# Twelve decoder layers: layer 0 in two stages instead of four, semaphores cleared seldom, layer 11's scores on row groups

## What is computed

```
y   = norm(x)                                   # (x - mean) / sqrt(var + 1e-5)
a   = norm(y) * ln1_g + ln1_b
q, k, v = a @ wq, a @ wk, a @ wv                # 16 heads of 8
phi(t)  = elu(t) + 1
kv, z   = sum_s phi(k) v^T, sum_s phi(k)        # per head
res = y + ((phi(q) kv) / (phi(q) z + 1e-6)) @ wo
h   = norm(res) * ln2_g + ln2_b
r   = clip(round((h @ w1) / 0.1), -128, 127) * 0.1
x   = x + res + gelu(r) @ w2                    # w1: 128 x 512
```

## Time and profile before

| | us |
|---|---|
| median of three runs | 2183.69 |
| lowest, highest | 2175.89, 2206.31 |
| the profiled execution | 2188.4 |
| its span, first to last instruction | 2186.6 |
| mean granted TensorE clock in it | 0.927 |
| layer 0, first to last instruction (timeline) | 13.05 to 123.24 |
| layer 11, first stage (timeline) | 2116.95 to 2179.35 |

### The profile page before, as it was taken

One profiled execution on the slowest core, in us unless ns is written; L12 is line 12 of the kernel. 1 busy time (PEld: TensorE's weight loads), 2 busy tenths in 40 slices (PEclk: granted clock), 3 DMA queues, 4 the chain that ended last, 5 costly groups with the idle time before them and its releaser, 6 DMA issues. The chain is left out here.

```text
span 2186.6 us, 51110 instructions
## 1 busy us (share of the span) xinstructions
PE 1934.8 (88%) x20189; PEld 1383.8 (63%) x20208; DVE 1409.9 (64%) x2480; ACT 1149.8 (53%) x2426; POOL 859.9 (39%) x1103
## 2 busy tenths in 40 slices
PE   4888999986657999999999877999899989999786
PEld 2435787862445688888888753788788856633332
DVE  3654887774575677777776433788778757934434
ACT  3444555554376766666665434555555551066452
POOL 0001454420144576656566200666566630044100
PEclk8998999997577999999999988999999988989898
DMA  6000110000001200000000040544344400000100
GB/s 279 1 1 1 50 39 30 30 10 0 1 1 58 108 23 13 22 13 22 13 22 23 13 184 4 145 127 132 114 126 129 132 30 1 1 1 1 43 1 21
DMA packets 31955, 107.54 MB, mean 49 GB/s; under 512 B 9440, under 2 KB 9568, under 8 KB 30816
## 3 DMA queue, kind: packets, MB, share of 16 engines
q1 hardware_dynamic: 30624, 104.07, 14.1%
q10 hardware_dynamic: 1088, 0.13, 0.0%
HBM read 94.16 MB, written 10.03 MB: 48 GB/s over the span
## 5 line engine op out<-in xcount | busy, mean ns | idle before, releaser
L600 PE MATMUL bank<-yh,wl 128*128 128x512 f32 x640 | 253.8, 396 | 15.2 <-DVE yl L1300 6.8
L602 PE MATMUL bank<-yh,wh 128*128 128x512 f32 x640 | 252.3, 394 | 0.0
L601 PE MATMUL bank<-yl,wh 128*128 128x512 f32 x640 | 251.9, 394 | 0.0
L1867 DVE SCALAR_TENSOR_TENSOR big<-bank,pack,big 128x256 f32<-128x256 f32 (+2 forms) x384 | 182.2, 477 | 34.2 <-ACT mask L1789 16.8
L1353 DVE TENSOR_TENSOR hl<-bank,hh 128x512 fp32r<-128x512 f32 x192 | 132.9, 692 | 68.5 <-ACT hh L1290 58.8
L1788 ACT ACTIVATE big<-bank,pack 128x256 f32<-128x256 f32 x192 | 91.1, 474 | 135.0 <-PE bank L1623 134.4
L1290 ACT ACTIVATE hh<-bank 128x512 fp32r<-128x512 f32 x192 | 115.3, 600 | 84.2 <-DVE bank L1348 82.7
L600 PEld LDWEIGHTS bank<-yh,wl 128*128 128x128 f32 x640 | 121.8, 190 | 50.7 <-issue 14.9
L688 ACT ACTIVATE a<-bank,pack 128x512 f32<-128x512 f32 x128 | 88.4, 691 | 105.8 <-PE bank L602 105.8
L592 POOL CAST wh<-big 128x384 fp32r<-128x384 f32 x64 | 61.1, 954 | 202.2 <-PE bank L602 135.9
L602 PEld LDWEIGHTS bank<-yh,wh 128*128 128x128 f32 x640 | 121.7, 190 | 26.7
(11 more groups left out here) (481 smaller groups left out, 4706.8 us busy)
## 6 DMA issues: line engine op xcount, KB each, us to landing
rep<-routing SPq DMA_DIRECT2D x64, 384.0 KB, 3.4
rep<-routing SPq DMA_DIRECT2D x64, 256.0 KB, 3.9
big<-in_big SPq DMA_DIRECT2D x1, 9216.0 KB, 25.6
rep<-routing SPq DMA_DIRECT2D x16, 512.0 KB, 3.6
gate<-big SPq DMA_DIRECT2D x32, 256.0 KB, 2.0
z<-gate SPq DMA_DIRECT2D x16, 512.0 KB, 3.4
rep<-routing SPq DMA_DIRECT2D x64, 128.0 KB, 3.6
big<-in_big SPq DMA_DIRECT2D x1, 6144.0 KB, 34.7
```

The lines of the kernel that those rows point to most:

```text
L600: nc.tensor.matmul(out, pl, dh[:, cur], start=start, stop=False)
L601: nc.tensor.matmul(out, ph, dl[:, cur], start=False, stop=False)
L602: return nc.tensor.matmul(out, ph, dh[:, cur], start=False, stop=stop)
L1867: ins = nc.vector.scalar_tensor_tensor(out=d, in0=conv_in(i, back), scalar=weight(i, 3 - back), in1=d, op0=ALU.mult, op1=ALU.add)
```

## The change

- Semaphores are cleared once more than 80 have been handed out since the last clear, and at the end of the program. The other stages end with the block's barrier alone.
- Layer 0 has two stages. The first norm moves into the attention stage, the second into the lookup stage. The double norm takes both factors from one variance v: Ln(v(1 + 1e-5) + 1e-10) and Ln(v + 1e-5), each with Exp of -0.5 times it. The banks are shared: states with values, output projection with denominator.
- In the lookup stage the middle rounding step and the sum of x and res are on GpSimd; r and g have four buffers, down is four units behind up. Batch 3 is normed in the middle of the units, with the Ln/Exp table loaded again.
- In layer 11, `Wc1` stands three times side by side, so that r appears on three groups of 32 rows, and `Wc2` is laid out in three groups of rows; each score matmul has its own row group. Down matmuls 0 to 2 are ahead of the small ones, 3 to 9 behind the scores. `base` signals `placed`, and GpSimd's sum of batch b waits for round b's `placed`.

```diff
@@ stage @@
-    nc.clear_and_free_semaphores(list(sems.values()))
-    nc.all_engine_barrier()
+    counted.extend(sems.values())
+    if len(counted) > 80:
+        zero(nc)
...
+def zero(nc):
+    nc.clear_and_free_semaphores(counted)
+    nc.all_engine_barrier()
+    counted.clear()
@@ l0_attention, banks and TensorE @@
+        xc, var, pk, pv, pq, pn, pd = k.ps[0:2], k.ps[2], k.ps[3], k.ps[4], k.ps[5], k.ps[6], k.ps[7]
+        pkv, po = pv, pd
...
+            def sums(b):
+                pe.wait_ge(s["kv_mask"], b + 1)
+                after(pe, s["done"], b)
+                nc.tensor.matmul(pd, zm[:, :], qe[b % 2][:, :], start=True, stop=True).then_inc(s["den"], 1)
+                after(pe, s["o_ready"], b)
+                nc.tensor.matmul(pn, kvm[:, :], qe[b % 2][:, :], start=True, stop=True).then_inc(s["den"], 1)
...
+            centre(0)
+            centre(1)
+            variance(0)
+            variance(1)
             for b in range(B + 1):
                 if b < B:
+                    project_in(b)
                 if b:
+                    sums(b - 1)
+                if b + 2 < B:
+                    centre(b + 2)
                 if b < B:
+                    states(b)
+                if b + 2 < B:
+                    variance(b + 2)
                 if b:
+                    project_out(b - 1)
@@ l0_attention, ScalarE @@
+            def invert(b):
+                r, t = rs[b % 2][:, :], ts[b % 2][:, :]
+                act.wait_ge(s["var"], b + 1)
+                after(act, s["y_ready"], b - 1)
+                nc.scalar.activation(t, var, ACT.Ln, scale=1.0 + 1e-5, bias=k.eps[1e-10]).then_inc(s["ln"], 1)
+                nc.scalar.activation(r, var, ACT.Ln, bias=k.eps[1e-5]).then_inc(s["ln"], 1)
+                act.wait_ge(s["ln"], 2 * b + 2)
+                nc.scalar.activation(t, t, ACT.Exp, scale=-0.5).then_inc(s["inv"], 1)
+                nc.scalar.activation(r, r, ACT.Exp, scale=-0.5).then_inc(s["inv"], 1)
...
                     nc.scalar.activation(rec[:, :], rec[:, :], ACT.Exp, scale=-1.0).then_inc(s["rec_ready"], 1)
+                if b + 2 < B:
+                    square(b + 2)
+                    invert(b + 2)
@@ l0_attention, VectorE @@
+            def normed(b):
+                dve.wait_ge(s["inv"], 2 * b + 1)
+                nc.vector.scalar_tensor_tensor(out=a[:, sl(b)], in0=xc[b % 2], scalar=k.w["L0_attn_ln1_g"], in1=ts[b % 2][:, :],
+                                               op0=ALU.mult, op1=ALU.mult).then_inc(s["gained"], 1)
+                dve.wait_ge(s["inv"], 2 * b + 2)
+                nc.vector.tensor_tensor(y[:, sl(b)], xc[b % 2], rs[b % 2][:, :], ALU.mult).then_inc(s["y_ready"], 1)
+                dve.wait_ge(s["gained"], b + 1)
+                nc.vector.tensor_scalar(a[:, sl(b)], a[:, sl(b)], k.w["L0_attn_ln1_b"], None, ALU.add).then_inc(s["a_ready"], 1)
...
                     nc.vector.scalar_tensor_tensor(out=ke[b % 2][:, :], in0=pk, scalar=0.0, in1=ke[b % 2][:, :], op0=ALU.max, op1=ALU.add).then_inc(s["k_phi"], 1)
+                    if b + 1 < B:
+                        normed(b + 1)
                     dve.wait_ge(s["q_exp"], b + 1)
@@ l0_lookup_mlp @@
+        @block.gpsimd
+        def _(pool):
+            for i in range(N):
+                cur = r[i % 4][:, :]
+                pool.wait_ge(s["rounded"], i + 1)
+                nc.gpsimd.tensor_scalar(cur, cur, MAGIC, -128.0, ALU.subtract, ALU.max).then_inc(s["low"], 1)
+                if i % C == C - 1:
+                    b = i // C
+                    nc.gpsimd.tensor_tensor(x[:, sl(b)], x[:, sl(b)], res[:, sl(b)], ALU.add).then_inc(s["added"], 1)
...
+            for i in range(N + 4):
+                if i < N:
+                    pe.wait_ge(s["h_ready"], i // C + 1)
+                    after(pe, s["rounded"], i - 2)
+                    nc.tensor.matmul(up_bank[i % 3], w1[:, sl(i % C, P)], y[:, sl(i // C)], start=True, stop=True).then_inc(s["up"], 1)
+                if i == 0:
+                    centre(2)
+                if i == 2:
+                    variance(2)
+                if i == 4:
+                    centre(3)
+                if i == 5:
+                    variance(3)
+                if i >= 4:
+                    down(i - 4)
...
+            invert(2)
+            for i in range(N):
+                if i == 2:
+                    nc.scalar.preload_act_table_set(LN_EXP)
+                    square(3)
+                    invert(3)
+                act.wait_ge(s["grid"], i + 1)
+                after(act, s["down"], i - 3)
+                nc.scalar.activation(g[i % 4][:, :], r[i % 4][:, :], ACT.Gelu_apprx_tanh).then_inc(s["act"], 1)
...
+            normed(0)
+            for i in range(N + 1):
+                if i < N:
+                    dve.wait_ge(s["up"], i + 1)
+                    after(dve, s["act"], i - 3)
+                    nc.vector.tensor_scalar(r[i % 4][:, :], up_bank[i % 3], 10.0, MAGIC, ALU.mult, ALU.add).then_inc(s["rounded"], 1)
+                if i == 0:
+                    normed(1)
+                if i == 1:
+                    normed(2)
+                if i == 5:
+                    normed(3)
+                if i:
+                    cur = r[(i - 1) % 4][:, :]
+                    dve.wait_ge(s["low"], i)
+                    nc.vector.tensor_scalar(cur, cur, 127.0, 0.1, ALU.min, ALU.mult).then_inc(s["grid"], 1)
+                if i % C == 2 and i > C:
+                    finish(i // C - 1)
@@ layer11 @@
                     pool.wait_ge(s["copied"], b + 1)
+                    pool.wait_ge(s["placed"], b + 1)
...
+                down(0)
                 pe.wait_ge(s["act"], B * FEW)
...
+                down(1)
                 pe.wait_ge(s["pooled"], 1)
...
+                down(2)
                 pe.wait_ge(s["r"], 1)
                 for j in range(3):
+                    rows = slice(j * R, (j + 1) * R)
+                    mm = nc.tensor.matmul(scores[:, sl(j)], r1[rows, :], k.big[rows, 2 * F:2 * F + S], start=True, stop=True, tile_position=(R * j, 0))
+                    mm.then_inc(s["scores"], 1)
-                for n in range(6):
+                for n in range(3, 10):
                     down(n)
...
-                    for i in range(6 + 2 * n, min(8 + 2 * n, B * FEW)):
+                    for i in range(10 + 2 * n, min(12 + 2 * n, B * FEW)):
...
-                    link(nc.vector.tensor_tensor(base[:, :], base[:, :], digit[:, :], ALU.bitwise_or))
+                    nc.vector.tensor_tensor(base[:, :], base[:, :], digit[:, :], ALU.bitwise_or).then_inc(s["placed"], 1)
```

More of the change, by code:

```diff
@@ L219, in _, with l0_lookup_mlp @@
             dve.wait_ge(s["done"], B)
-def l0_lookup_mlp(nc, k, h, y, x):
+def l0_lookup_mlp(nc, k, res, y, x):
     C = 4
-    with ExitStack() as mem, stage(nc, "up rounded grid act down chain done") as (block, s):
+    N = B * C
+    names = "centred squared var ln inv h_ready added up rounded low grid act down done chain"
+    with ExitStack() as mem, stage(nc, names) as (block, s):
         sb = lambda n, w: mem.enter_context(nc.sbuf_tensor(f"{n}_{nc.next_id()}", [P, w], F32))
-        r, g = sb("r", 3 * S), sb("g", 3 * S)
+        r, g = [sb("r", S) for _ in range(4)], [sb("g", S) for _ in range(4)]
+        sq, rs = ([sb(n, S) for _ in range(2)] for n in ("sq", "rs"))
@@ L230, in _, with centre, variance @@
         @block.tensor
         def _(pe):
+            def centre(b):
+                after(pe, s["h_ready"], b - 1)
+                nc.tensor.matmul(xc[b % 2], k.w["centre"], res[:, sl(b)], start=True, stop=True).then_inc(s["centred"], 1)
+            def variance(b):
+                pe.wait_ge(s["squared"], b + 1)
+                after(pe, s["ln"], b)
+                nc.tensor.matmul(var, k.mean, sq[b % 2][:, :], start=True, stop=True).then_inc(s["var"], 1)
             def down(i):
@@ L245, in _ @@
-            down(B * C - 1)
-        def finish(dve, link, b):
-            dve.wait_ge(s["down"], C * (b + 1))
-            link(nc.vector.tensor_tensor(y[:, sl(b)], y[:, sl(b)], k.ps[4 + b % 2][:, :], ALU.add))
-            nc.vector.tensor_tensor(x[:, sl(b)], x[:, sl(b)], y[:, sl(b)], ALU.add).then_inc(s["done"], 1)
+                nc.tensor.matmul(down_bank[b % 2], w2[:, sl(c, P)], g[i % 4][:, :], start=c == 0, stop=c == C - 1).then_inc(s["down"], 1)
+            centre(0)
+            centre(1)
@@ L265, in _, with normed @@
-            finish(dve, link, B - 1)
-        @block.scalar
-        def _(act):
-            for i in range(B * C):
-                act.wait_ge(s["grid"], i + 1)
-                after(act, s["down"], i - 2)
-                nc.scalar.activation(g[:, sl(i % 3)], r[:, sl(i % 3)], ACT.Gelu_apprx_tanh).then_inc(s["act"], 1)
+            def normed(b):
+                dve.wait_ge(s["inv"], b + 1)
```

(11 more changed lines are left out.)

179 lines of the change are left out of this document (103 added, 76 removed).

## The result

The changed kernel took 2167.26 us, the median of 20 runs (2155.79 to 2182.54), beside 2188.54 for the kernel before (20 runs, 2173.75 to 2206.31). The ratio is 0.9894 [0.9865, 0.9922], that is 23 us less with an interval of 17 to 30; the two medians themselves lie 21.3 apart. The forecast was 24.3 less, 2159.4, in a range of 2138 to 2184. The total came out about as forecast. Its parts did not, and the largest one failed.

A forecast was written before the change was run, and what follows sets the result against it. TensorE is busy 88%, but layer 0 and layer 11 are chains through engines, and all engines stand about 0.95 us at stage ends. Gains 6.9 + 11.9 + 5.5 = 24.3 off the median 2183.69 give 2159.4 us, range 2138 to 2184.

The forecast's parts named there:

- Boundaries, 6.9: Stage ends outside layer 0: 16 without a clear save 0.45 us each, less a few tenths; 6.9 us, bounds 0 and 8.3.
- rival B: Stage ends give nearly nothing, a lone barrier drains as long, and layer 11 stays at the low clock: 2168; chance 0.14.
- Layer 0, 11.9: Layer 0's two merged stages and their ends: layer 1 starts at 112.4 against 124.32, a gain of 11.9 us.
- First stage, 51.6: Layer 0's merged norm and attention: 9.45 until the first batch is ready, then four batches and tail, 51.6 us.
- The wait of the third batch: Layer 0's attention: the denominator shares a bank with the projection, so waits for VectorE's residual add; batch 10.95 against 7.65.
- one such stretch: Layer 0's second stage: TensorE stands before Gelu 2, then runs at 1.2 GHz for a while; about 1.7 us.
- Second stage, 47.2: Layer 0's merged norm and lookup: 43.9 us, plus 1.6 for VectorE waiting on GpSimd and 1.7 for low clock.
- GpSimd's one-input step: Lookup's middle rounding step on GpSimd: in no row, taken as 1.0 us, between a cast's 0.67 and a two-input op's 1.31.
- Rival A: GpSimd sets the lookup's pace, every clamp waiting for it and the reverse: 2.6 us a unit, total 2170; chance 0.13.
- The three table loads: Layer 0's second stage: three ScalarE activation table loads, a switch costing 1.30 us with no drain.
- Layer 11, 5.5: Layer 11: scores side by side 3.4 net, totals off the rounds' VectorE steps 2.4, `base` 0.5; 5.5 taken, bounds 3.6 and 6.3.
- Rival D: Stretches at 1.2 GHz after 16 stage ends vanish with shorter gaps: 27 us more gain, 2132; chance 0.08.

The follow-up runs named there:

- only_clears: The kernel before with only the seldom semaphore clears added: 2176.5 us against 2189.9, ratio 0.9938 [0.9905, 0.9971].
- low_split: Changed kernel with the lookup's middle rounding step alternating, even units on GpSimd, odd on VectorE: 2148.80 us, one run; second stage 6.6 us shorter.
- low_on_vector: Changed kernel with the lookup's middle rounding step back on VectorE, x + res still on GpSimd: 2154.11 us, one run; second stage 45.96 us.
- one_op: Changed kernel with GpSimd's rounding step only subtracting, the clamp at -128 left out: 2168.59 us, one run; second stage 47.12 us.
- totals_unplaced: Changed kernel with GpSimd's totals in layer 11 not waiting for `placed`: 2176.79 us, one run; stage 57.41 us, 1.0 longer.
- downs_behind: Changed kernel with layer 11's down matmuls 0 to 2 behind the scores again, row groups kept: 2161.40 us, one run; stage 59.94 us, 3.5 longer.
- clears_back: Changed kernel with a semaphore clear at every stage end again: 2176.86 us, ratio to the kernel before 0.9937 [0.9907, 0.9966].
- best: Changed kernel with add_early and low_split together: 2142.03 us, median of six runs, beside 2197.11 for the kernel before; ratio 0.9757 [0.9721, 0.9792].
- add_early: Changed kernel with VectorE's residual add ahead of the key clamp in layer 0's attention: 2159.26 us, one run; first stage 44.27 us.

## Why the prediction was right in its total and wrong in layer 0

- **Boundaries, 6.9: right.** Most bare ends have a gap of 0.45 to 0.50, as foretold, and the gaps behind layer 0 are 5.6 shorter in sum. Too small was "a few tenths go back if a longer clear costs more": it was about 1.6, 0.1 to 0.55 at each of four clears. That boundaries give nothing (half of rival B) fell with only_clears.
- **Layer 0, 11.9: wrong, 2.95 in the pair of traces, and not told from zero by the timed runs.** Two terms failed.
  - *First stage, 51.6, was 56.07.* The sum was sound at full clock: low_split ran the same code in 50.51. The wait of the third batch was seen and placed rightly, and also the fourth's. What was missing is a term for stretches near 1.2 GHz at the waits. I had priced one such stretch, in the second stage, and none here; three came in this execution, for 4.5 to 5.6 us. They come in most executions and not in all, so this term is a matter of chance as well.
  - *Second stage, 47.2, was 51.46.* The failed step is "GpSimd's one-input step ... I take 1.0", bounds 0.67 and 1.31; it took 1.91 to 2.09. I took the rate of a cast and of a two-input sum as ends for another kind of instruction. Four steps and a sum are 4 x 2.0 + 1.26 = 9.3 us, or 2.33 a unit, as the starts of the sums say too, where I had 1.9 and TensorE needs 1.72. The start was even better than foretold: the third Gelu at 20.8 in place of 22.35. From there 30.7 us went by in place of 24.9.
  - low_on_vector, one_op and low_split show the price as the cause. The unit goes with it: 2.33 us with a step of 1.99, 1.90 with one of 1.59, and TensorE's 1.72 with GpSimd's step in every other unit. The stage goes with the unit: 51.46, 47.12, 44.89.
- **Rival A** had this mechanism, GpSimd as the pace of the lookup, with 2.6 a unit and 2170. The place was right, the reason half: GpSimd's own time makes 2.33; the mutual waiting adds to VectorE (clamps 860 ns in place of 427) but not to the pace. In absolute time its 2170 is nearer to 2167.26 than my 2159.4; as a difference to the kernel before (13.7 less) it is farther from 23 than my 24.3. Of the SBUF page of the Trainium skill ("Who interferes with whom") the rule that such a VectorE operation and GpSimd exclude each other agrees with the rows: the clamp is 0.41 alone, 1.48 from just after GpSimd's sum to just after its end.
- **The three table loads: right.** The second load is at 84.08 and the next activation at 85.38, 1.30 later as in the earlier trace rows. The drain of which the ScalarE page of the Trainium skill speaks ("What ACT_TABLE_LOAD costs") is not seen here either.
- **Layer 11, 5.5: right, 6.0**, with 7 by the timed runs. Its parts trade places: three downs ahead are worth 3.5, row groups 1.6, totals behind `placed` 1.0. I had charged the downs as a cost that the clock might return; they are the largest gain. With them the clock is 1.00 through the scores, without them 0.50, and fewer downs stand in front of the first round. Taken singly the three make 6.1.
- **The 8.6 us of unchanged stages: not forecast.** They make up for layer 0's failure, and no term of the sum stood for them. That the total fitted is luck to that extent. Layer 9's attention, windows of before and then of after:

```profile
1788.08:2052.03 263.95, 245.43 (x2192) 129.18 (x2208) 156.36 (x154) 100.05 (x157) 64.82 (x146) 0.91 0.00 1
```

```profile
1783.69:2036.33 252.64, 236.96 (x2208) 122.46 (x2208) 156.13 (x154) 99.94 (x157) 64.57 (x146) 0.95 0.00 1
```

  The same instructions, 0.91 and 0.95 of the clock. In the other traces this stage was 252.6 to 269.4 long, and no edit goes with it: long in totals_unplaced, short in downs_behind and clears_back. But the mean granted clock of a whole execution does go with the kernel: its median is 0.923 in 35 runs of the kernel before (0.915 to 0.927), 0.9315 in only_clears, 0.9345 in 20 runs of the changed kernel (0.927 to 0.939), 0.9415 in best. Within the runs of the kernel before, 0.01 of clock goes with 16 us. By that 0.0115 more clock would go with 19 us (an estimate), so most of the 23 us shows as clock. In part that is the edits themselves: TensorE's long idle in the old first norm also reads 0.50 (26 to 38 us), and layer 11's first stage went from 0.84 to 0.87. Rival D, that more low stretches vanish than I see, may hold for a part of it. How much, and why in layer 9, stays open: nothing here held the clock still while the rest changed.

## What to carry to other kernels

Price an instruction that is moved to another engine by a row of the same kind on that engine; where there is none, put the upper end well above the nearest other kind, since here even the one-operation form took 1.59 us where the two-input sum takes 1.26. When two results share a bank, put the instruction that frees the bank ahead of the long steps on its engine: the move of four lines was worth 6.2 us at an equal clock, more than the rest of layer 0's change. And compare stage by stage, the unchanged ones too: the total alone would have called layer 0 a success, and add_early and one_op failures.

## What the runs showed of the hardware that was not expected

- GpSimd's tensor_scalar on 128x512 float32 takes 1.99 us with two operations and 1.59 with one; its tensor_tensor takes 1.26, and VectorE does the two-operation form in 0.42.
- A clear grows with the number of semaphores: the ends behind layers 5, 7 and 10 took 1.10, 1.09 and 1.08 with the stage's own 30 or 31, and 1.57, 1.61 and 1.63 with 97, 108 and 110, about 7 ns a semaphore. The end of layer 2's norm went from 1.36 with 10 to 1.46 with 85 only, which is not explained.
- At layer 0's three long TensorE waits (1.25 to 3.42 us) a granted clock of 0.51 to 0.64 followed for about 4 us in the changed kernel's trace, although TensorE was busy then. In low_split the same three waits were followed by 1.00 throughout: the same code was 50.5 us long or 56.
- One stage of unchanged code, layer 9's attention, was 252.6 to 269.4 us long from one execution to the next, as its granted clock went (0.95 to 0.89); the largest single difference between two profiled executions can thus lie where nothing was changed.
